# A three-stage kernel: the dead states' product moved from VectorE to GpSimd, the residual sum and two attention queues reordered

## What is computed

```
uc = silu(conv(u));   x_dbl = uc @ Wx;   dt = softplus(x_dbl[:16] @ Wdt + bdt)
h  = exp(dt * A) * h + (dt * uc) * B          # 32 states for each channel
y  = sum over states of h * C;   y = y + uc * Dp;   y = y * silu(z);   out = y @ Wout
```

## Time and profile before

| What | us |
|---|---|
| median of 3 runs | 4272.15 (4269.27 to 4273.1) |
| the profiled execution, its own time | 4265.17 |
| span of its profile | 4263.7 |
| PE busy | 3975.5 (93%) |
| DVE busy | 3651.0 (86%) |
| ACT busy | 2806.3 (66%) |
| POOL busy | 2313.7 (54%) |

### The profile page before, as it was taken

How to read it: one execution, slowest core, us unless ns; L and a number is a source line. 1 busy time by engine, 2 the same in 40 slices (tenths; PEclk the granted TensorE clock), 3 DMA queues, 4 the chain that set the end, 5 groups by cost and what they waited for, 6 DMA issues and landing times. The chain is left out here.

```text
span 4263.7 us, 69826 instructions
## 1 busy us (share of the span) xinstructions
PE 3975.5 (93%) x19212; PEld 3002.5 (70%) x19213; DVE 3651.0 (86%) x6958; ACT 2806.3 (66%) x4602; POOL 2313.7 (54%) x1949
## 2 busy tenths in 40 slices
PE   6999999999999999999999779999999699999998
PEld 4666666666666666666666557888887488888887
DVE  7999999999999999999999758887888666666665
ACT  5777777777777777777777656665666344454454
POOL 2554545454554545454554546666666555555555
PEclk8988998898989998898989888888889699999999
DMA  2122211222222221122222212222222355555555
GB/s 70 47 46 43 53 43 43 42 53 43 50 46 43 53 43 44 42 53 43 50 46 43 47 45 93 78 78 79 80 77 76 128 93 86 96 102 97 84 95 85
DMA packets 198461, 272.58 MB, mean 64 GB/s; under 512 B 23377, under 2 KB 143058, under 8 KB 198354
## 3 DMA queue, kind: packets, MB, share of 16 engines
q0 software_dynamic: 94432, 130.60, 17.2%
q1 hardware_dynamic: 100480, 138.48, 11.6%
q10 hardware_dynamic: 3442, 2.21, 0.2%
HBM read 121.07 MB, written 150.14 MB: 64 GB/s over the span
## 5 line engine op out<-in xcount | busy, mean ns | idle before, releaser
L615 PE MATMUL pj<-xt,win 128*128 128x512 f32 x3144 | 937.6, 459 | 95.6 <-DVE uc L803 63.0
L615 PEld LDWEIGHTS pj<-xt,win 128*128 128x128 f32 x3144 | 686.9, 222 | 325.6 <-DVE uc L803 89.8
L1992 POOL DMA_INDIRECT out<-e_y,e_to x272 | 473.3, 1740 | 365.4 <-ACT e_y L2098 305.7
L803 DVE SCALAR_TENSOR_TENSOR uc<-pj,convw,uc 128x511 f32<-128x511 f32 (+2 forms) x780 | 516.7, 728 | 5.4 <-ACT uc L408 5.4
L301 POOL TENSOR_TENSOR r<-r,neg_half 128x4 f32<-128x4 f32 x64 | 75.9, 1186 | 760.7 <-ACT r L384 760.7
L326 POOL TENSOR_TENSOR wk<-v,uc 128x512 f32<-128x512 f32 x260 | 333.2, 1281 | 281.3 <-DVE v L851 280.5
L663 PE MATMUL po<-yz,wout 128*128 128x512 f32 x1024 | 456.5, 599 | 4.6 <-ACT fb L491 4.6
L2043 PE MATMUL e_p<-e_w,e_a 128*128 128x256 f32 x3264 | 416.4, 284 | 0.8 <-DVE e_a L2153 0.8
L2043 PEld LDWEIGHTS e_p<-e_w,e_a 128*128 128x128 f32 x3264 | 393.8, 188 | 11.1 <-DVE e_a L2153 2.8
L2031 PE MATMUL e_p<-e_xt,e_w 128*128 128x512 f32 x1632 | 395.1, 397 | 4.1 <-DVE e_xt L2145 2.4
L663 PEld LDWEIGHTS po<-yz,wout 128*128 128x128 f32 x1024 | 189.3, 190 | 267.8 <-issue 267.8
(11 more groups left out here) (244 smaller groups left out, 9105.5 us busy)
## 6 DMA issues: line engine op xcount, KB each, us to landing
e_x<-expert_in SPq DMA_DIRECT2D x138, 260.0 KB, 2.6
bb<-bc SPq DMA_DIRECT2D x65, 512.0 KB, 5.6
h_rows<-fb POOLq DMA_DIRECT2D x64, 512.0 KB, 6.3
h_rows<-h0c SPq DMA_DIRECT2D x32, 512.0 KB, 2.9
a_h<-h_rows SPq DMA_DIRECT2D x128, 128.0 KB
out<-a_bs SPq DMA_DIRECT2D x128, 128.0 KB
bc<-xd SPq DMA_DIRECT2D x65, 128.0 KB, 2.3
e_w1s<-in_moe_w POOLq DMA_DIRECT2D x9, 512.0 KB, 5.5
```

The source lines that it names most:

```text
L615: i = mm(pj[m][:], win[d][wp][:, k, c:c + P], xt[xp][:, k, :], start=(k == 0 and n == 0), stop=(k == KD - 1 and n == 2))
L803: stt(uc[d][:, m, to], pj[m][:, of], convw[d][:, m, tap:tap + 1], uc[d][:, m, to], ALU.mult, ALU.add).then_inc(S["cv"], 1)
L1992: pool.indirect_dma_start(out=out, out_offset=bass.IndirectOffsetOnAxis(ap=to[n][:, j:j + 1].bitcast(U32), axis=0), in_=y[n][:, j, :], in_ ...
```

## The change

**On DVE**, dead_part is gone. sums becomes tp = qq * dall + tp (two operations of 1024 columns), a new function direct adds uc * Dp (four operations of 512 columns) between sums and gate, and outputs moves ahead of bc_product. **On POOL**, dead_inputs computes qq = wk * S in four operations of 512 columns for each step; keep_residual moves from the odd half of the loop, ahead of gather, into the even half, between the second and third tile of scan_inputs. **On ACT**, sum_copy copies S from PSUM to SBUF (`ssum`). **In attention**, POOL sends a chunk's eight scatters in groups of two, four and two at three places of its slot instead of together, and PE runs turn2 between the second and the third part of qk.

```diff
@@ -318,10 +319,10 @@
-            def scan_inputs(t, d):
+            def scan_inputs(t, d, tiles=range(MD)):
                 pool.wait_ge(S["bcast"], 16 * (t + 1))
-                for m in range(MD):
+                for m in tiles:
                     pool.wait_ge(S["dt_ok"], t + 1)
@@ -329,6 +330,13 @@
+            def dead_inputs(t):
+                for m in range(MD):
+                    pool.wait_ge(S["dtu_ok"], MD * t + m + 1)
+                    pool.wait_ge(S["sc_ok"], t + 1)
+                    pool.tensor_tensor(qq[:, m, :], wk[:, m, :], ssum[:], ALU.mult).then_inc(S["pq_ok"], 1)
             gather(0)
@@ -340,15 +348,19 @@
                         ln_scale(s + 1)
+                    dead_inputs(t)
                     if not first:
...
                         row_scale(t - 1)
-                    if d == 1:
+                    if d == 0:
+                        scan_inputs(t + 1, 1, range(2))
+                        keep_residual(s + 1)
+                        scan_inputs(t + 1, 1, range(2, MD))
+                    else:
                         pool.wait_ge(S["gt_ok"], 2 * t + 4)
-                        keep_residual(s + 1)
                         gather(s + 2)
-                    scan_inputs(t + 1, 1 - d)
+                        scan_inputs(t + 1, 0)
@@ -431,7 +443,6 @@
                     if not (isinstance(t, int) and t == 0):
-                        act.wait_ge(S["q_ok"], NP * (t - 1) + m // 2 + 1)
                         act.wait_ge(S["dtu_ok"], MD * (t - 1) + m + 1)
@@ -459,6 +470,7 @@
                         act.wait_ge(S["tp_ok"], MD * (t - 1) + 2 * h + 2)
+                        act.wait_ge(S["pq_ok"], MD * (t - 1) + 2 * h + 2)
                     act.activation(wk[:, mm, :], y[:, mm, :], ACT.Identity, bias=1.0).then_inc(S["w_ok"], 1)
@@ -471,6 +483,13 @@
                     act.activation(y[:, m, :], v[:, m, :], ACT.Exp, scale=amat[d][:, m, 0:1]).then_inc(S["da_ok"], 1)
+            def sum_copy(t):
+                act.wait_ge(S["s_ps"], t + 1)
+                if not (isinstance(t, int) and t == 0):
+                    act.wait_ge(S["pq_ok"], MD * t)
+                act.activation(ssum[:], pss[:], ACT.Copy).then_inc(S["sc_ok"], 1)
@@ -525,6 +544,7 @@
                 last_tap_and_bias(t + 1, 1 - d, range(MD))
+                sum_copy(t)
                 if copies:
@@ -668,7 +688,7 @@
                 if not last:
-                    pe.wait_ge(S["q_ok"], NP * (t + 2))
+                    pe.wait_ge(S["sc_ok"], t + 2)
                 for j in range(TT):
@@ -858,19 +878,6 @@
-            def dead_part(t, d):
-                dve.wait_ge(S["s_ps"], t + 1)
-                dve.wait_ge(S["fl_ok"], 3 * t + 2)
-                for h, mm in pairs():
-                    stt(qq[:, mm, :], over_pair(pss[:]), dall[:], v[:, mm, :], ALU.mult, ALU.mult
-                        ).then_inc(S["q_ok"], 1)
-                for m in range(MD):
-                    dve.wait_ge(S["q_ok"], NP * t + m // 2 + 1)
-                    stt(qq[:, m, :], qq[:, m, :], dp[d][:, m:m + 1], uc[d][:, m, :], ALU.add, ALU.mult
-                        ).then_inc(S["q2_ok"], 1)
@@ -898,8 +905,8 @@
                             dve.wait_ge(S["e_hc"], at)
-                            dve.wait_ge(S["q2_ok"], MD * (t + 1))
-                            tt(qq[:, m, :], qq[:, m, :], eh, ALU.add).then_inc(S["e_y"], 1)
+                            dve.wait_ge(S["hc_ok"], t + 1)
+                            tt(tp[:, m, :], tp[:, m, :], eh, ALU.add).then_inc(S["e_y"], 1)
                         dve.reg_add(dve_count, dve_count, 1)
@@ -908,10 +915,18 @@
+                dve.wait_ge(S["fl_ok"], 3 * t + 2)
                 for h, mm in pairs():
                     dve.wait_ge(S["hc_ok"], t + 1)
-                    dve.wait_ge(S["q2_ok"], MD * t + 2 * h + 2)
-                    tt(tp[:, mm, :], tp[:, mm, :], qq[:, mm, :], ALU.add).then_inc(S["yv_ok"], 1)
+                    dve.wait_ge(S["pq_ok"], MD * t + 2 * h + 2)
+                    stt(tp[:, mm, :], qq[:, mm, :], dall[:], tp[:, mm, :], ALU.mult, ALU.add).then_inc(S["yv_ok"], 1)
+            def direct(t, d):
+                for m in range(MD):
+                    dve.wait_ge(S["yv_ok"], NP * t + m // 2 + 1)
+                    stt(tp[:, m, :], uc[d][:, m, :], dp[d][:, m:m + 1], tp[:, m, :], ALU.mult, ALU.add
+                        ).then_inc(S["q2_ok"], 1)
@@ -919,7 +934,7 @@
                 for h, mm in pairs():
-                    dve.wait_ge(S["yv_ok"], NP * t + h + 1)
+                    dve.wait_ge(S["q2_ok"], MD * t + 2 * h + 2)
                     tt(yz[:, mm, :], tp[:, mm, :], zs[d][:, mm, :], ALU.mult).then_inc(S["yz_ok"], 1)
@@ -947,14 +962,14 @@
                         ln_stats(s + 1)
-                    dead_part(t, d)
                     scan(t, d)
+                    outputs(t, d)
                     bc_product(t + 1, 1 - d)
-                    outputs(t, d)
                     more_states(t, d)
...
                     sums(t)
+                    direct(t, d)
                     gate(t, d)
@@ -1268,10 +1283,10 @@
-            def send(c):
+            def send(c, tiles=range(TT)):
                 wait_apart(pool, (S["rt"], ROUTES * (c + 1)))
-                for j in range(TT):
+                for j in tiles:
                     for k in range(TOP):
@@ -1319,16 +1334,21 @@
                     scales2(c - 1)
+                    if c > 2:
+                        send(c - 3, (3,))
                     base(c - 1)
                 normalise(c)
+                if c >= 2:
+                    send(c - 2, (0,))
                 if c + 2 < NCH:
                     scales1(c + 2)
-                if not (isinstance(c, int) and c < 2):
-                    send(c - 2)
+                if c >= 2:
+                    send(c - 2, (1, 2))
...
             scales2(NCH - 1)
+            send(NCH - 3, (3,))
             base(NCH - 1)
@@ -1463,10 +1483,10 @@
-            def qk(c):
+            def qk(c, parts=range(QT)):
                 pe.wait_ge(S["lt_ok"], KD * (c + 1))
-                for t in range(QT):
+                for t in parts:
                     if t == 2:
@@ -1573,9 +1593,12 @@
                 if c + 1 < NCH:
-                    qk(c + 1)
+                    qk(c + 1, range(2))
                 if not (isinstance(c, int) and c == 0):
                     turn2(c - 1)
+                if c + 1 < NCH:
+                    qk(c + 1, (2,))
+                if not (isinstance(c, int) and c == 0):
                     if not (isinstance(c, int) and c < 2):
                         ranks(c - 2)
```

More of the change, by code:

```diff
@@ L121, in mamba_stage @@
         qq = sb("qq", [P, MD, SEQ])
+        ssum = sb("ssum", [P, SEQ])
         tp = sb("tp", [P, MD, SEQ])
@@ L145, in mamba_stage @@
           u_ps a_ok z_ps z_ok uc_ok xd_ps xd_ok bc_ok bcast xd_st dt_ps v_ok vc_ok y_ok l_ok w_ok g_ok
-          d0_ok dt_ok dtu_ok tp_ok da_ok h_ok hc_ok q_ok q2_ok yv_ok yz_ok xm_ok qd_ps gt_ok ct_ok cnt_ps
+          d0_ok dt_ok dtu_ok tp_ok da_ok h_ok hc_ok sc_ok pq_ok q2_ok yv_ok yz_ok xm_ok qd_ps gt_ok ct_ok cnt_ps
           fl_ok s_ps o_ps fo_ok sq_ok ss_ps rv_ok rr_ok f_ps fin_ok h1_st acc gt2 e_bc e_da e_tp e_h e_hc e_y""".split()
@@ L653, in state_sum @@
                 if not (isinstance(t, int) and t == 0):
-                    pe.wait_ge(S["q_ok"], NP * t)
+                    pe.wait_ge(S["sc_ok"], t)
                 mm(pss[:], smask0[:], bcp[:], start=True, stop=True).then_inc(S["s_ps"], 1)
```

## The result

The changed kernel takes **4522.14 us** (median of 4 runs, 4508.86 to 4530.2); the kernel before took 4271.56 (4 runs, 4269.27 to 4273.1) beside it. The ratio is 1.0591, with a 95% interval of 1.0562 to 1.062: 5.9% slower. The profiled execution took 4508.86 us (span 4507.3).

The account below looks back on a forecast made before the run. DVE sets the scan stage's pace, PE close behind, with even slots pinned at xt_low. Odd +3.1 and even +6.6 make +9.7 a pair, times 32 +310; attention -25; from 4265.2 to 4550, plus 7 is 4557 us, range 4500 to 4610.

Parts of the forecast that it names:

- a pin at xt_low: Even slot: DVE's xt_low waits for ACT's copy, which hangs on ln_apply behind POOL's ln_scale; at +23.85 us before the change.
- faster: Rival, scan stage: products and direct hide, the wait moves forward, PE bounds; 4192 us, chance 0.08.
- The unknown: Scan stage: whether POOL also holds DVE's scans and outputs, or only they hold POOL; worth 200 us; forecast assumed both.
- only DVE holds POOL: Rival, scan stage: POOL doesn't hold scans or outputs; +3.1 us for each pair of slots, 4346 us, chance 0.14.
- Even slot: +6.6: Scan stage, each even slot: grows to 43.8 us, 2.66 from direct and 3.95 from the late ln_scale.
- direct's 2.66: Even slot: direct lies behind DVE's wait at xt_low, where dead_part lay ahead of it, and costs 2.66 us.
- ln_scale's 3.95: Even slot: POOL's small operations wait for whole DVE instructions, ending at +20.5 instead of +16.44, costing 3.95 us.
- Small operations slip through: Rival, even slot: POOL and DVE take turns, but ln_scale is only some 2 us late; 4493 us, chance 0.14.
- Odd slot: +3.1: Scan stage, each odd slot: POOL and DVE take turns on two-tile operations; 39.6 us instead of 36.5.
- 8.1 + 10.4 + 7.3: Odd slot: POOL's work until the residual sum ends, its remaining eight operations, DVE's scans, outputs and half of sums; 25.8 us.
- Residual sum: Odd slot: its stall of DVE, 2.3 us, goes from each pair of slots because it now runs beside the convolution.
- Attention: -25: Attention stage: turn2's new place may make the clock fall less often; middle between nothing and 50 us saved.

Follow-up runs that it names:

- e9: The changed kernel with bc_product put back ahead of outputs on DVE: 4442.57 us, 1.0414 to the kernel before.
- e11: The changed kernel with POOL's ln_scale ahead of the fourth tile of the even slot's scan_inputs: 4411.7 us, 1.0332 to the kernel before.
- e3: The changed kernel with direct moved behind bc_product, ahead of xt_low, and sums after it: 4421.12 us, 1.0366 to the kernel before.
- e4: The changed kernel with POOL's four dead products cut to 4 columns each, leaving them out of the result: 4448.1 us, 1.0408 to the kernel before.
- e1: The changed kernel's scan stage with the attention and expert stages of the kernel before: 4526.33 us, 1.0612 to the kernel before.
- e5: The changed kernel with keep_residual put back where it was, ahead of gather: 4511.61 us, 1.058 to the kernel before.
- e2: The scan stage of the kernel before with the changed kernel's attention stage: 4240.93 us, 0.9937 to the kernel before.
- e8: The kernel before with only attention's scatters in groups, PE's order as before: 4254.47 us, 0.9978 to the kernel before.
- e6: The kernel before with the residual sum in quarters, two for each slot, started after the scans beside bc_product: 4199.28 us, 0.9861.
- e12: The changed kernel with both ln_scale ahead of the fourth scan_inputs tile and direct ahead of xt_low: 4444.63 us, 1.0405 to the kernel before.

## Why the prediction was right, step by step

- **What bounds the kernel.** DVE in the scan stage with a pin at xt_low: right, and the rival "faster" falls with it. From ln_apply to sums it is 8.47 us again (1065.26 to 1073.73). The even slot went down where an edit touched what releases the pin (e9, e11) or what lies behind it (e3), and not where the dead products went (e4).
- **Who holds whom.** The unknown that was worth 200 us. Scans (1.198 to 1.893 us on the mean) and outputs (2.29 to 3.17) are held by POOL too, one whole instruction in turn. This is the direction that no row before showed for the scan; the rival "only DVE holds POOL" falls with it. The Trainium skill, SBUF — State Buffer, section Who interferes with whom, has a VectorE instruction with two SBUF inputs and a GpSimd instruction that reads SBUF block each other. The trace agrees for the scan: 2.21 us beside POOL's products instead of 1.20.
- **Even slot: +6.6, measured +6.45.** ln_scale was to end at +20.5 and ended at +20.22; xt_low starts at +27.53, sums at +28.73 (29.0). Of the two terms, direct's 2.66 was measured alone (2.65, e3). Of ln_scale's 3.95, outputs in front of the power is 2.1 (e9). e11 moved all of ln_scale forward and hit DVE's own limit after 3.2, so the full term is read from the trace (3.78, 20.22 - 16.44) and not from a run. "Small operations slip through" falls: 0.99, 1.03 and 3.16 us.
- **Odd slot: +3.1, measured +1.9.** The mis-sized term is 8.1 + 10.4 + 7.3, the end of the last dead product. I had it at +25.8 with half of sums ahead of it, so at +24.7 without. No half of sums ran ahead; that alone changes nothing, since the half then stands behind. But the last product ends at +23.57 (1112.20). POOL works on from +7.83 (1096.46, not 8.1) to there, with one gap of 0.16, 15.7 us: 10.0 of its own (4 x 1.27 and 4.94, not 10.4) and 5.7 behind four scans and outputs (not 6.15). So each term of the turns was a little too long, and the mechanism was right. From there to the end of the slot it is 14.8 as summed; the 0.1 of hand-over losses isn't there.
- **The total.** The scan stage lost 261 us (e1) where the sum has 310: 32 x 1.2 = 38 of the 49 are the odd slot, 32 x 0.15 = 5 the even one, the rest I can't place. Attention gave 10 in the whole kernel where the sum has 25. The two errors have opposite signs, and 4557 missed 4522 by only 35 because they offset each other in part.
- **PE.** The projection waits for bc_product as foreseen; PE's waits for it are 61.1 us over 26, new, and hidden in the slot: e9 has bc_product 3.2 us earlier in the odd slot, which stays at 38.4.
- **Residual sum.** The 2.3 us taken out were booked as a gain that its place undoes; e5 shows that the move is worth nothing.
- **Attention: -25.** Measured alone -25 (e2), and that the number fits is luck: it was the middle between nothing and 50 us for turn2's effect on the clock, and that turn2 makes the clock fall less often is not shown. What is shown is the other part: the scatters in groups shorten a fast slot by some 1.7 us, about one of the three waits of 2 us that I had put down for them, and give 9 us alone (e8). How many slots are fast changes from run to run. The changed kernel lost 251 us on its chip and e1 261, so in most of its runs some 10 us of attention's gain arrived.

## What to carry to other kernels

Work moved to GpSimd is not taken from VectorE where VectorE's instructions beside it read two SBUF tiles: here 8.6 us for each pair taken off VectorE came back as 9.8 us of turns and waits. But look at the place of the work before its amount: the moved products themselves cost 2.6 us of a pair's 8.3 (e4), and what they and the new order put behind or in front of one wait, direct and ln_scale, cost 6.4; 0.7 was gained in the odd slot. Give GpSimd's large operations the time in which VectorE reads PSUM or waits, as e6 does for 1.4%. Ask of each small operation of GpSimd which VectorE instruction stands before it, since here it waited for the whole of it. And gains from shortening two sides of one wait do not add (e12).

## What the runs showed of the hardware

- A scan of 512 columns with two SBUF inputs takes 1.20 us alone (mean before the change) and 2.21 beside a GpSimd product.
- A GpSimd operation on 4 columns takes 0.20 us free and 0.99 in turn with scans; the power on 4 columns takes 3.16 behind outputs against 1.05 beside bc_product.
- DVE's operations with two SBUF inputs beside a train of GpSimd products don't double: outputs, 2.29 us alone, takes 3.17, and sums 3.18 instead of 2.47: 0.9 and 0.7 us longer, less than the 1.27 of one product. Neither lost more than one turn here, though outputs is a single long instruction and sums are two.
